# Two attention layers: GpSimd takes halves of mean and variance and the scaling by 1/std, keys of both groups in their own buffers, batches written out

## What is computed

```python
# layer 0: 8 heads of 32 channels, 1024 x 1024 scores a head
mean, var = x.mean(axis=1), x.var(axis=1)            # over the channels
xn = (x - mean) / sqrt(var + 1e-5) * gamma
q, k, v = split(einsum('oc,bcn->bon', w_qkv, xn))
sim = einsum('bhdi,bhdj->bhij', q, k) * 32**-0.5 + bias[None]
x = einsum('oc,bcn->bon', w_out, softmax(sim) @ v) + x
# layer 1: one head, f and g with 32 channels, h with 256
f, g, hh = Wf @ x + bf, Wg @ x + bg, Wh @ x + bh
out = gamma1 * (hh @ softmax(f^T g)) + x
```

## Time and profile before

| | us |
|---|---|
| median of 3 runs | 1881.58 (1879.25 to 1883.2) |
| span of the profiled execution | 1881.0 |
| PE busy | 1642.2 (87%) |
| DVE busy | 1498.6 (80%) |
| ACT busy | 1388.9 (74%) |
| GpSimd busy | 0.2 |
| first row tile starts (batch 0) | 122.2 |
| batch 4, its first row tile to that of batch 5 | 968.5 to 1183.3 |
| first row tile of batch 7 | 1612.4 |

### The profile page before, as it was taken

How to read it: one execution, slowest core, us unless ns; L and a number is a source line. 1 busy time by engine, 2 the same in 40 slices (tenths; PEclk the granted TensorE clock), 3 DMA queues, 4 the chain that set the end, 5 groups by cost and what they waited for, 6 DMA issues and landing times. The chain is left out here.

```text
span 1881.0 us, 23267 instructions
## 1 busy us (share of the span) xinstructions
PE 1642.2 (87%) x6545; PEld 805.5 (43%) x6545; DVE 1498.6 (80%) x2218; ACT 1388.9 (74%) x2043; POOL 0.2 (0%) x4
## 2 busy tenths in 40 slices
PE   6645989989988998989988999889989999889988
PEld 2133343535444453535444353535435354435424
DVE  4235988888878988789878989789878988789853
ACT  1135887878778887788778787778778787779853
POOL 0000000000000000000000000000000000000000
PEclk8667968999999999999999999999999999989999
DMA  1395103301042104301043102501043101500000
GB/s 57 58 221 156 33 25 105 110 19 39 24 138 77 57 1 127 111 1 57 24 108 107 57 1 85 149 5 57 1 128 110 43 15 53 142 20 26 16 30 23
DMA packets 72905, 123.04 MB, mean 65 GB/s; under 512 B 24042, under 2 KB 38954, under 8 KB 72746
## 3 DMA queue, kind: packets, MB, share of 16 engines
q1 hardware_dynamic: 72756, 121.29, 22.7%
HBM read 78.66 MB, written 44.13 MB: 65 GB/s over the span
## 5 line engine op out<-in xcount | busy, mean ns | idle before, releaser
L1117 DVE CUSTOM_DVE_ANT_0 biased<-psum,bias_lines_sb 128x1024 f32<-128x1024 f32 x512 | 618.0, 1222 | 209.1 <-issue 129.1
L915 ACT ACTIVATE biased<-biased,nmax 128x1024 f32<-128x1024 f32 x512 | 587.2, 1147 | 188.9 <-DVE nmax L1117 183.7
L1131 DVE TENSOR_TENSOR biased<-psum,bias_lines_sb 128x1024 f32<-128x1024 f32 x512 | 599.1, 1221 | 47.7 <-PE psum L715 37.1
L932 ACT ACTIVATE probs<-biased 128x1024 f32<-128x1024 f32 x512 | 536.0, 1056 | 132.7 <-DVE biased L1131 118.8
L688 PE MATMUL psum<-k_tail,q_stack 96*128 96x256 f32 x512 | 272.8, 533 | 120.3 <-DVE nmax L1117 50.6
L715 PE MATMUL psum<-q_stack,k_main 98*128 98x512 f32 x768 | 302.9, 502 | 38.9 <-DVE nmax L1117 15.1
L742 PE MATMUL psum<-probs,vT 128*32 128x512 f32 x2048 | 292.6, 642 | 4.9 <-DVE st L1008 2.7
L715 PEld LDWEIGHTS psum<-q_stack,k_main 98*128 98x128 f32 x768 | 137.2, 205 | 257.9 <-issue 112.6
L688 PEld LDWEIGHTS psum<-k_tail,q_stack 96*128 96x128 f32 x512 | 102.8, 201 | 305.7 <-DVE nmax L1117 172.5
L690 PE MATMUL psum<-k_main,q_stack 96*128 96x512 f32 x512 | 216.3, 422 | 0.0
L633 PE MATMUL psum<-probs 128*128 128x512 f32 x384 | 186.6, 592 | 0.0
(11 more groups left out here) (91 smaller groups left out, 1409.2 us busy)
## 6 DMA issues: line engine op xcount, KB each, us to landing
q_stack<-q_parts SPq DMA_DIRECT2D x96, 256.0 KB, 5.6
k_parts<-st SPq DMA_DIRECT2D x16, 1024.0 KB, 4.7
q_parts<-st SPq DMA_DIRECT2D x16, 1024.0 KB, 4.0
k_main<-k_parts SPq DMA_DIRECT2D x48, 256.0 KB, 5.3
xn<-in_x_dram SPq DMA_DIRECT2D x8, 1024.0 KB, 8.6
x<-in_x_dram SPq DMA_DIRECT2D x8, 1024.0 KB, 11.2
out_dram<-x SPq DMA_DIRECT2D x8, 1024.0 KB, 4.0
bias_lines_sb<-bias_lines SPq DMA_DIRECT2D x32, 240.0 KB, 20.6
```

What stands on the lines that cost most here:

```text
L915: nc.scalar.activation(biased[:, m % BIASED, :], biased[:, m % BIASED, :], ACT.Exp, scale=-1.0, bias=nmax[:, m:m + 1], accum_out=rowsum[:, ...
L932: nc.scalar.activation(probs[:, n % P_SLOTS], biased[:, n % BIASED, :] .rearrange("p (i n) -> p i n", i=2), ACT.Exp).then_inc(SEMS["probs_ ...
L1117: nc.vector.tensor_tensor_reduce(biased[:, m % BIASED, :], pair(bank_of(g, first, ("rows", m))), bias_lines[:, g * HG + h, a0:a0 + N], -1. ...
L1131: nc.vector.tensor_tensor(biased[:, n % BIASED, :].rearrange("p (i n) -> p i n", i=2), psum[:, bank:bank + 2, :], bias_lines[:, g * HG + 2 ...
```

## The change

- `mean` and `var`: GpSimd first adds the two channel halves (`sum_x` at step 18, `sum_squares` at step 25), PE multiplies the sum in two halves in place of four quanta (`mean` at steps 22 and 23, `var` at 28 and 29).
- `norm` is issued by GpSimd instead of DVE, at the same steps. The same holds for batch 0 in the setup.
- Keys: `k_stack` holds all 1024 positions for both groups; a load is three DMAs of 512 KB in place of nine. A row tile is two matmuls of 512 columns in place of 256, 256 and 512.
- SP's order: the store and the load of k of group 1 stand right behind q's, ahead of the load of x. The key loads wait for the store and for the columns of the batch before.
- `batches` is written out, eight times the body; waits have constants, and the start values of the counters go.

```diff
-        KMAIN = 3 * N // 4
-        k_main = sb("k_main", [KS + 2, HG, KMAIN], F32R)
-        k_tail = sb("k_tail", [KS + 2, G, HG, N - KMAIN], F32R)
+        k_stack = sb("k_stack", [KS + 2, G, HG, N], F32R)
...
+        x_sum, square_sum = squares[:, 1, :], squares[:, 0, :]
...
-        K_DMAS = 3 * 3 * 16
+        K_DMAS = 3 * 16
...
-            value = b * per_batch[name] + (start[name] + n)
...
+            value = b * per_batch[name] + n
+            if value > 0:
                 eng.wait_ge(SEMS[name], value)
...
-        side_0 += [(20 + i, "mean", i) for i in range(QUANTA)] + [(23, "centre", 0), (24, "square", 0)]
+        side_0 += [(18, "sum_x", 0), (22, "mean", 0), (23, "mean", 1), (23, "centre", 0), (24, "square", 0)]
+        side_0 += [(25, "sum_squares", 0)]
         side_0 += [(24 + i, "f", i) for i in range(QUANTA)] + [(27, "high_f", 0), (29, "low_f", 0)]
-        side_0 += [(27 + i, "var", i) for i in range(QUANTA)] + [(30, "rstd", 0)]
+        side_0 += [(28, "var", 0), (29, "var", 1), (30, "rstd", 0)]
...
-        def batches(eng, body):
-
-            body(0, first=True, last=False)
-            with eng.Fori(1, B - 1) as b:
-                body(b, first=False, last=False)
-            body(B - 1, first=False, last=True)
+        def batches(body):
+            for b in range(B):
+                body(b, first=(b == 0), last=(b == B - 1))
...
-            def k_in(b, g, chunk):
+            def k_in(b, g):
 
                 need(sp, "k_stored", b, 16 * (g + 1))
-                cols = slice(KCHUNKS[chunk], KCHUNKS[chunk + 1])
-                dst = k_main[:, :, cols] if cols.start < KMAIN else k_tail[:, g]
+                need(sp, "s_mm", b - 1, (g + 1) * SN)
                 for r, part in enumerate((0, 1, 0)):
-                    sp.dma_start(dst[r * HD:(r + 1) * HD].bitcast(F32),
-                                 k_dram.ap()[part, :, :, cols].rearrange("h d n -> d h n")).then_inc(k_loaded, 16)
+                    sp.dma_start(k_stack[r * HD:(r + 1) * HD, g].bitcast(F32),
+                                 k_dram.ap()[part].rearrange("h d n -> d h n")).then_inc(k_loaded, 16)
...
             def element(b, first, last):
                 q_out(b, 1)
                 q_in(b, 1, ("s_mm", b, 0))
+                k_out(b, 1)
+                k_in(b, 1)
                 if not last:
 
                     need(sp, "v_mm", b, NT)
                     need(sp, "qk_mm", b, split(1, 1))
                     sp.dma_start(xn[:], x_dram[b + 1]).then_inc(x_loaded, 16)
-                k_out(b, 1)
-                k_in(b, 1, 2)
                 for r in range(NHALF):
                     shift_to_stack(b, 0, r)
-                for chunk in range(2):
-                    columns_done(b, 0, chunk)
-                    k_in(b, 1, chunk)
                 if not last:
                     k_out(b + 1, 0)
-                    need(sp, "s_mm", b, SN)
-                    k_in(b + 1, 0, 2)
+                    k_in(b + 1, 0)
...
-                if kind == "mean":
-                    if arg == 0:
-                        need(pe, "x_loaded", b, 16)
+                if kind in ("mean", "var"):
+                    if arg == 0 and kind == "mean":
                         need(pe, "lo_ready", b - 1, split(1, 1))
-                    product(arg, 6, lambda k: mean_w[:], xn, "mean_mm")
-                elif kind == "var":
-                    if arg == 0:
-                        need(pe, "squared", b, KC)
-                    product(arg, 6, lambda k: mean_w[:], squares, "var_mm")
+                        need(pe, "x_summed", b, 1)
+                    elif arg == 0:
+                        need(pe, "squares_summed", b, 1)
+                    src = x_sum if kind == "mean" else square_sum
+                    mm = pe.matmul(psum[:, 6 + arg, :], mean_w[:], src[:, arg * HALF:(arg + 1) * HALF],
+                                   start=True, stop=True)
...
-                pe.matmul(psum[:, bank, 0:keys], lhsT, tail[:, ::-1], start=True, stop=True)
-                pe.matmul(psum[:, bank, keys:HALF], lhsT, back(main, 0, HALF - keys, KMAIN), start=True, stop=True)
-                pe.matmul(psum[:, bank + 1, :], lhsT, back(main, HALF - keys, HALF, KMAIN), start=True,
+                keys = k_stack[0:KS, g, h, :]
+                pe.matmul(psum[:, bank, :], lhsT, back(keys, 0, HALF, N), start=True, stop=True)
+                pe.matmul(psum[:, bank + 1, :], lhsT, back(keys, HALF, HALF, N), start=True,
...
+        @block.gpsimd
+        def _(pool):
+            def do(kind, arg, b):
+                if kind == "sum_x":
+                    need(pool, "k_stored", b - 1, 16 * G)
+                    need(pool, "x_loaded", b, 16)
+                    nc.gpsimd.tensor_tensor(x_sum, xn[:, 0, :], xn[:, 1, :], ALU.add).then_inc(SEMS["x_summed"], 1)
+                elif kind == "sum_squares":
+                    need(pool, "squared", b, KC)
+                    nc.gpsimd.tensor_tensor(square_sum, squares[:, 0, :], squares[:, 1, :],
+                                            ALU.add).then_inc(SEMS["squares_summed"], 1)
+                elif kind == "norm":
+                    if arg == 0:
+                        need(pool, "centered", b, KC)
+                        need(pool, "rstd_ready", b, 2)
+                    nc.gpsimd.tensor_tensor(xn[:, arg, :], xn[:, arg, :], rstd, ALU.mult).then_inc(SEMS["normed"], 1)
```

More of the change, by code:

```diff
@@ L194, in two_layer_attention @@
                       rows_ready=G * NHALF, probs_ready=G * TG * HP, o_ready=G * NHALF, fg_hi=3, e1_ready=NT, hs_ready=NT)
-        for kind in (TENSOR, VECTOR, SCALAR):
+        for kind in (TENSOR, VECTOR, SCALAR, POOL):
             for name, n in kind.items():
@@ L266, in two_layer_attention @@
                    "exp1", "invert", "scale_h", "sa", "add_y")
-        AHEAD = ("mean", "centre", "square", "var", "rstd", "norm", "q0", "high_q0", "low_q0", "k0", "high_k0",
+        AHEAD = ("sum_x", "mean", "centre", "square", "sum_squares", "var", "rstd", "norm", "q0", "high_q0", "low_q0", "k0", "high_k0",
                  "low_k0")
@@ L338, in column_tile @@
             return half, t, j
-        KCHUNKS = (0, N // 2, KMAIN, N)
         LEAD = 3
@@ L355, in _ @@
         def _(sp):
-            for name in ("x_loaded", "res_loaded", "q_stored", "q_loaded", "k_stored", "k_loaded", "rows_loaded",
-                         "y_stored"):
-                sp.sem_inc(SEMS[name], start[name])
             sp.dma_start(xn[:], x_dram[0]).then_inc(x_loaded, 16)
@@ L444, in _ @@
             q_out(0, 0)
-            for chunk in (2, 0, 1):
-                k_in(0, 0, chunk)
+            k_in(0, 0)
             q_in(0, 0, ("s_mm", -1, SN))
@@ L484, in element @@
                     q_in(b + 1, 0, ("s_mm", b, SN))
[L485 to L488, removed]
                 residual_in(b)
-            batches(sp, element)
+            batches(element)
             result_out(B - 1)
-            sp.wait_ge(y_stored, 16 * (B + 1))
+            sp.wait_ge(y_stored, 16 * B)
         @block.tensor
         def _(pe):
-            for name in TENSOR:
-                pe.sem_inc(SEMS[name], start[name])
             pe.wait_ge(weights_loaded, 16 * N_WEIGHTS)
@@ L714, in columns_phase @@
                             for i in range(2):
-                                mm = pe.matmul(psum[:, bank + i, :], key_tile(g, 2 * j + i, t),
+                                mm = pe.matmul(psum[:, bank + i, :], k_stack[:, g, 2 * j + i, t * P:(t + 1) * P],
                                                q_stack[:, g, NHALF - 1 - half, 2 * j + i, ::-1],
@@ L772, in _ @@
                     if step == at:
-                        for quantum in range(QUANTA):
-                            do(kind, quantum, 0, 1, True, False)
+                        for half in range(NHALF):
+                            do(kind, half, 0, 1, True, False)
             pe.wait_ge(table_ready, MSTEPS)
@@ L786, in element @@
                     columns_phase(b, g, first, last)
-            batches(pe, element)
+            batches(element)
             for kind, arg, b in alone(LAYER_1):
@@ L794, in _ @@
             nc.scalar.preload_act_table_set("natural_log_exp_and_others")
-            for name in SCALAR:
-                act.sem_inc(SEMS[name], start[name])
             def do(kind, arg, b, g, first, last, tail=False):
                 if kind == "square":
-                    need(act, "k_stored", b - 1, 16 * G)
                     for k in range(KC):
@@ L940, in element @@
                     output(b, 1, 1, last)
-            batches(act, element)
+            batches(element)
             for kind, arg, b in alone(LAYER_1):
                 do(kind, arg, b, 1, False, False, tail=True)
+        @block.gpsimd
[14 more added lines that the diff above has]
+                    nc.gpsimd.tensor_tensor(xn[:, arg, :], xn[:, arg, :], rstd, ALU.mult).then_inc(SEMS["normed"], 1)
```

(29 more changed lines are left out.)

29 lines of the change are left out of this document (5 added, 24 removed).

## The result

The changed kernel takes 1936.06 us (median of 4 runs, 1934.94 to 1937.73), the kernel before 1881.53 us in the same comparison. The ratio is 1.0293, with a 95% interval of 1.0279 to 1.0308: **slower by 54.5 us**, where 20 us were forecast and 1922 was the end of the range. The profiled execution spans 1935.6 us.

What follows compares the result with a forecast made beforehand. No engine fills the span; the bound changes by phase, and PE waits for keys at every change of batch (32.8 us). Terms -47 - 2 + 81 + 6 - 9 - 8 = +21 gave 1902 us, range 1866 to 1922.

Steps and rivals of the forecast that it cites:

- part 4: Norm on GpSimd: DVE saves 16 us, meeting the shift steps costs 7 us (1 us a batch); together -9 us.
- Part 1: Batch boundaries: whole key buffers remove PE's wait for keys, -47 us; merging the row tile's matmuls, -2 us.
- Part 2: Row phase of group 0: x lands late behind the key loads, PE waits at the mean; +81 us.
- Part 3: Row tiles 24 to 29: GpSimd's add of the squares delays the variance, +0.9 us, 7 times; +6 us.
- Part 5: Setup: half the mean and variance matmul time goes, norm leaves DVE, counters' start values go; -8 us.
- rest: Stretches outside the other terms (group 1, batch 7, its second layer): forecast difference 0.
- rival 2: GpSimd's norm holds up DVE's shift instructions for its whole length: 1929 us, at half of it 1915; chance 0.12.
- Rivals 1 and 3: Rival 1: x comes sooner, 1866 us, chance 0.20; rival 3: shorter wait, full boundary gain, 1883 us, chance 0.08.

Runs made afterwards that it cites:

- e3: Changed kernel with norm still on GpSimd, but waiting until DVE is through with the shift steps: 1909.52 us, ratio 1.0155 to the kernel before.
- e6: Kernel before with whole key buffers for both groups, hardware loop kept: 1838.1 us, ratio 0.9765.
- e5: Kernel before with the eight batches written out in place of the hardware loop: 1867.15 us, ratio 0.9927.
- e1: Changed kernel with the load of x back ahead of the store and load of k: 1857.38 us, ratio 0.987 to the kernel before.
- e7: As e4, but the variance as four matmul quanta on PE, without GpSimd's add of the squares: 1819.09 us, ratio 0.9666 to the kernel before.
- e2: Changed kernel with norm back on DVE, in the setup too: 1918.52 us, ratio 1.0201 to the kernel before.
- e8: Changed kernel with x loaded first and nothing on GpSimd; key buffers and written-out batches stay: 1824.91 us, ratio 0.9729 to the kernel before.
- e9: As e8, plus norm on GpSimd behind the shift steps, in the batches alone: 1814.41 us, ratio 0.9642 to the kernel before.
- e4: Changed kernel with the edits of e1 and e3 together: 1830.8 us, ratio 0.9735 to the kernel before.

## Why the prediction was wrong

Slower was right and the largest term too, but the sum came to +21 where +54.5 was measured, outside the range. The step that failed is in part 4: the forecast put the meeting of GpSimd's norm and DVE's shift steps at 1 us a batch, and it cost 4.1 (e3 against the changed kernel). By its own steps:

- **Part 1, keys: right.** -49 forecast with the merged matmul, -52.4 measured; e6 and e5 show 42.8 for the buffers and 9.8 for the loop. The queries were late next, as said, by 0.62 us and not felt. Merging the row tile's matmuls shows no gain where it can be seen alone: row tile 4 of group 1 to its columns is 368.0 before and 369.3 after.
- **Part 2, x behind the keys: right**, +83.2 for +81, and e1 takes 81.6 of it back. PE's seven waits were 11.2 us on average, 10.3 in batch 4, where "8 to 10" was forecast. The working held too: x landed at 16.4 us for 16, the add took 2.34 us for 2.4, and from PE's restart to tile 24 it took 1060.04 - 1053.37 = 6.7 us for 6.8. The Trainium skill's figure (GPSIMD Engine Reference, section 3.1) had given an estimate of 2.25 us.
- **Part 3, variance: mechanism right, size wrong.** The variance began 1066.93 - 1060.04 = 6.9 us behind tile 24, as forecast. The step that failed is "with it (0.85), the row tile (0.48)": those are times at the full clock, and PE had just waited. Behind the wait the granted clock was 0.64, and from the variance's start to tile 29 it took 1069.38 - 1066.93 = 2.45 us where the terms make 1.5. So tile 29 came 9.3 us behind tile 24 and not 8.4. Twice the forecast, +11.7 for +6. e7, without the add and the wait, takes 11.8 back.
- **Part 4, norm: the step that failed most.** "I take 1 us a batch, +7, nearer to nothing since they are short" had nothing to stand on. In these traces the length of the held-up instruction doesn't set the hold-up; what is left of the GpSimd instruction that it meets does (0.17 us became 0.90 and 2.28). e3 against the changed kernel gives 4.1 us a batch for my 1, near the upper end (4.8) that I had written down. The saving was over-rated as well: two instructions of 1.21 us off DVE gave 9.9 us in 7 batches (e2 to e3) or 11.6 (e8 to e9) and not 16; DVE's busy time fell in full (43.4 us to 41.3 in e9's batch 4), but the phase did not follow it all the way, and no run here says which of its waits took the rest. Forecast -9, measured +18.5: 27.5 of the 34 us that were missing. Of them 21.8 are the meeting (28.8 for 7) and about 6 the saving. Part 5's 10.7, part 3's 5.7 and part 2's 2.2 add to the gap; the keys and "rest" took 12.4 back. This is rival 2, held at 0.12; the rule that it named was there to be read, and the two places (norm from step 3, shift steps at step 4) as well.
- **Part 5, setup: the gain didn't come.** The mean's matmuls fell from 6.02 to 3.78 us, by 2.2 and not by half (3.0). The same exclusion then took the rest: the setup's L1034 and L1041 have two SBUF operands and normally take 0.6 us. DVE in the changed kernel, the first beside the add of the squares, the others beside norm:

```profile
37.21 2.34 DVE L1034 SCALAR_TENSOR_TENSOR bias_lines_sb<-bias_lines_sb 64x441 f32<-64x441 f32 x1 [1.64 <-ACT bias_lines_sb L820]
...
51.88 2.41 DVE L1034 SCALAR_TENSOR_TENSOR bias_lines_sb<-bias_lines_sb 64x441 f32<-64x441 f32 x1 [1.41 <-ACT bias_lines_sb L820]
54.22 2.75 DVE L1041 SCALAR_TENSOR_TENSOR bias_lines_sb<-bias_lines_sb 64x441 f32<-64x441 f32 x1
```

  They lose (2.34 - 0.61) + (2.41 - 0.61) + (2.75 - 0.61) = 5.7 us, more than the 4.3 that PE saved (the variance's matmuls fell from 5.83 to 3.78). With norm off DVE, the two kernels are level at the end of the chain to the bias table. SP issues the store of the table (L437, now L386) at 68.70 us before and at 68.96 after. The other 2.4 us come behind it, in the chain of small DMAs that part 5 counted at nothing. The +2.7 itself can't be read as a loss: the four kernels with the changed setup (after, e1, e3, e4) start their first row tile at 122.1 to 125.0.
- **The rest**, put at nothing, was -9.0, of which 7.5 is the changing length of the columns of group 1, with no cause shown. Without this luck the forecast would have been further off.

Rivals 1 and 3 fell: the key loads ran at the lower rate throughout. Rival 2 had the mechanism, and its 1929 us is still 7 below the 1936 measured. With x first, the same change is 1.3% faster than the kernel before (e1), so the sign hung on one place in SP's queue.

## What to carry to other kernels

Before work moves to GpSimd, list the DVE instructions that will run beside it and have two SBUF inputs. Here even one of 0.17 us was held for nearly a whole GpSimd instruction (2.28 us), and letting GpSimd wait for them cost less than meeting them. In a queue that works in order, put the load with the nearest use first, and ask of each load made earlier what it now stands in front of. Behind a new wait, look in the trace for the clock at which PE restarts, and cost its next matmuls at that clock.

## What was not expected of the hardware

- The exclusion goes by whole instructions: 0.17 us steps became 0.90 and 2.28 us and ended 0.1 us or less behind the GpSimd instruction that they met. GpSimd lost nothing by it in the batches (4.69 us for its two, 4.71 in e3 beside tiles alone). In the setup it did: its two norm instructions, against the longer L1034 and L1041, took 5.01 us. DVE's tiles, with one operand in PSUM, were untouched: the 512 row tiles have a mean of 1221 ns in the kernel after, with GpSimd's adds beside some of them, and in e9, without.
- A hardware loop's turn is not free: some 1.5 us at the first tile of a batch (e6), and 9.8 us in all over the changes of batch when it goes (e5).
- A store of 1 MB takes 3.9 us from issue to landing behind idle queues, but 7.3 us in e1, where it was issued while x was being loaded.
